# Second attention: scores of two query tiles as 64-row products in both halves of the TensorE array, keys block-diagonal for pairs of heads

## The reference, cut to what matters

```python
def _L1_xattn_ref(x, cond, wq, bq, wkv, bkv, wp, bp):     # x, cond: 16 x 128 x 512
    q = _qdq(x) @ _qdq(wq).T + bq                          # int8 fake-quantised
    k, v = jnp.split(cond @ wkv.T + bkv, 2, axis=-1)
    q, k, v = (t.reshape(B, 128, 16, 32) for t in (q, k, v))
    attn = jax.nn.softmax(jnp.einsum('bnhd,bmhd->bhnm', q, k) * scale, axis=-1)
    o = jnp.einsum('bhnm,bmhd->bnhd', attn, v).reshape(B, N, C)
    return _qdq(o) @ _qdq(wp).T + bp
x = x + _L1_xattn_ref(_layernorm(x), ctx_2048, ...)
```

## Time and profile before

| what | value |
|---|---|
| median of three runs | 1466.27 us |
| the runs | 1461.33, 1466.27, 1466.6 us |
| span of the profiled execution | 1463.7 us |
| second attention, first to last score product | 768.1 to 1037.4 us of the span |
| PE busy over the span | 93% |
| DVE, ACT busy over the span | 69%, 54% |

### The profile page before, as it was taken

One profiled execution on the slowest core, in us unless ns is written; L12 is line 12 of the kernel. 1 busy time (PEld: TensorE's weight loads), 2 busy tenths in 40 slices (PEclk: granted clock), 3 DMA queues, 4 the chain that ended last, 5 costly groups with the idle time before them and its releaser, 6 DMA issues. The chain is left out here.

```text
span 1463.7 us, 28639 instructions
## 1 busy us (share of the span) xinstructions
PE 1354.5 (93%) x8666; PEld 813.1 (56%) x8666; DVE 1002.8 (69%) x3234; ACT 791.5 (54%) x1802; POOL 249.2 (17%) x265
## 2 busy tenths in 40 slices
PE   3678999999999799999989999999789999999998
PEld 1345555555555444444455555555434777777774
DVE  8889999999997646456546788887659654545211
ACT  4777888888888733332357677776530233332331
POOL 4100000000000100000010000002411255555552
PEclk7699999999999999999999999999999999999999
DMA  8534344343440300000020000000322588888885
GB/s 261 145 87 99 91 107 106 86 119 90 107 104 17 145 1 0 0 0 0 0 75 15 16 16 14 14 1 2 146 85 93 184 247 251 255 257 246 255 233 115
DMA packets 63186, 149.52 MB, mean 102 GB/s; under 512 B 10792, under 2 KB 27830, under 8 KB 58892
## 3 DMA queue, kind: packets, MB, share of 16 engines
q1 hardware_dynamic: 49836, 115.70, 26.1%
q0 software_dynamic: 13280, 32.93, 9.6%
HBM read 113.21 MB, written 35.39 MB: 102 GB/s over the span
## 5 line engine op out<-in xcount | busy, mean ns | idle before, releaser
L776 DVE CUSTOM_DVE_ANT_0 masked_scores<-ps_max,band_mask 128x192 bf16<-128x192 f32 (+1 forms) x512 | 177.2, 383 | 20.5 <-PE ps_max L505 13.9
L383 ACT ACTIVATE probs_t<-ps_sc 128x448 f32<-128x448 f32 x256 | 138.7, 542 | 80.4 <-PE ps_sc L525 78.1
L1255 PE MATMUL f_ps<-f_xt,w_t 128*128 (+1 forms) x704 | 160.2, 382 | 2.5 <-ACT w_t L1310 2.5
L377 ACT ACTIVATE nf_above<-nf_scaled,nf_sign_at 128x512 f16<-128x512 bf16 x231 | 161.5, 715 | 0.0
L2803 DVE TENSOR_TENSOR d_inter<-d_silu_g,d_su 128x384 f32<-128x384 f32 x32 | 17.7, 554 | 159.6 <-PE d_su L2487 154.4
L1927 ACT ACTIVATE c_probs<-d_sg,c_negmax 128x128 f32<-128x128 f32 x256 | 90.3, 365 | 58.1 <-DVE c_negmax L2012 57.7
L1255 PEld LDWEIGHTS f_ps<-f_xt,w_t 128*128 128x128 bf16 x704 | 69.3, 98 | 86.7 <-issue 5.0
L2320 POOL DMA_INDIRECT out<-d_h,d_scatter_now x64 | 97.2, 1519 | 108.3 <-DMA out<-d_h,d_scatter_now 92.9
L505 PE MATMUL ps_max<-k_stack,q_stack 96*128 96x192 bf16 (+1 forms) x512 | 96.5, 272 | 19.8 <-DVE row_max L776 13.8
L2671 DVE TENSOR_SCALAR d_onehot<-d_slot_no,d_pos 128x192 bf16<-128x192 bf16 x512 | 101.0, 288 | 0.3 <-PE d_lb L2388 0.3
L505 PEld LDWEIGHTS ps_max<-k_stack,q_stack 96*128 96x128 bf16 x512 | 46.2, 101 | 92.1 <-issue 46.9
(11 more groups left out here) (381 smaller groups left out, 2830.1 us busy)
## 6 DMA issues: line engine op xcount, KB each, us to landing
d_wgu<-in_ex_gu SPq DMA_DIRECT2D x32, 1024.0 KB
d_wdown<-in_ex_d SPq DMA_DIRECT2D x32, 512.0 KB
dr_parts<-qk_parts SPq DMA_DIRECT2D x32, 384.0 KB, 4.8
q_stack<-dr_parts SPq DMA_DIRECT2D x32, 192.0 KB, 2.7
k_stack<-dr_parts SPq DMA_DIRECT2D x32, 192.0 KB, 3.3
out<-x_sb SPq DMA_DIRECT2D x21, 256.0 KB, 2.2
nf_w<-in_nf_w POOLq DMA_DIRECT2D x3, 1408.0 KB, 10.2
q_stack<-dr_parts SPq DMA_DIRECT2D x32, 128.0 KB, 2.4
```

The lines of the kernel that those rows point to most:

```text
L377: act.activation(above[:, g, k, :], lvl[:, g, :], ACT.Sign, bias=cut[:, k - NDV:k - NDV + 1]).then_inc(s_sg, 1)
L383: act.activation(pt[:, c, :], SP[c % 2][:].rearrange("p a w -> p (a w)")[:, a:z], ACT.Exp, scale=D0 ** -0.5).then_inc(s_e, 1)
L776: op = dve.tensor_tensor_reduce(masked[:, c % 2, k, off:off + hi - lo], M[c % 2][:, k, off:off + hi - lo], mask[:, k, off:off + hi - lo], ...
L1255: mm = pe.matmul(bank[:], w12[:, m, kt, ft * P:(ft + 1) * P], xt[:, q, kt, bass.ds(g * N, N)], start=(kt == 0 and q == 0), stop=(kt == KT ...
```

## The change

One product of scores now covers two heads instead of four: the keys in `kbd` are block-diagonal only within pairs of heads, so a tile of 128 features by 128 keys shrinks from four key blocks (512 columns) to two (256 columns), and rows 0 to 63 and rows 64 to 127 are used by separate products, each with 64 rows and 256 columns. `score_pair` issues the four of them for two neighbouring tiles, `ot` and `ot + 1`: those of the lower half of the rows write bank `SB[0]`, those of the upper half bank `SB[1]`. A bank therefore holds two heads of two tiles. The pair waits until all exponentials before it are done, since it fills both banks. The number of maxima is as before (two for two tiles, each over a whole bank), and so are the exponentials and the transposes; what each exponential reads is another place.

On ScalarE the key copies of steps 0 and 4 now stand behind the exponentials of steps 1 and 5, together with those of these steps (`key_piece`), and `q_bias(g, 1)` behind the exponentials of step 1 instead of step 0. The two buffers of keys are half as large, so the memsets that zero them are too.

```diff
-            def scores(n, par, bb, ot):
-                ge(pe, s_ex, n - 1)
-                pe.matmul(SB[ot % 2][:], qt[:, par, ot, bb * P:(bb + 1) * P], kbd[par][:, ot, bb, :, :],
-                          start=True, stop=True).then_inc(s_S, 1)
+            def score_pair(n, par, bb, ot):
+
+                ge(pe, s_ex, n)
+                for o in range(2):
+                    for a in range(2):
+                        rows = slice(64 * a, 64 * a + 64)
+                        mm = pe.matmul(SB[a][:, 2 * o:2 * o + 2, :], qt[rows, par, ot + o, bb * P:(bb + 1) * P],
+                                       kbd[par][rows, ot + o, bb, :, :], start=True, stop=True, skip_group_check=True)
+                        if o == 1:
+                            mm.then_inc(s_S, 1)
...
-                        if bb == 0 and ot % 2 == 0:
-                            pe.wait_ge(s_qb, 2 * g + ot // 2 + 1)
-                        scores(n, par, bb, ot)
+                        if ot % 2 == 0:
+                            if bb == 0:
+                                pe.wait_ge(s_qb, 2 * g + ot // 2 + 1)
+                            score_pair(n, par, bb, ot)
...
-                    op = act.activation(kbd[par][rows, ot, :, j, :],
+                    op = act.activation(kbd[par][rows, ot, :, j % 2, :],
...
-                        act.wait_ge(s_nm, n + 1)
+                        if ot % 2 == 0:
+                            act.wait_ge(s_nm, n + 1)
                         ge(act, s_T, n - 1)
...
                         for j in range(4):
-                            op = act.activation(pr[:, ot % 2, j, :], SB[ot % 2][:, j, :], ACT.Exp, bias=nm[:, ot % 2, j:j + 1],
+                            if ot % 2 == 0 and j == 2:
+                                act.wait_ge(s_nm, n + 2)
+                            at = 2 * (ot % 2) + j % 2
+                            op = act.activation(pr[:, ot % 2, j, :], SB[j // 2][:, at, :], ACT.Exp, bias=nm[:, j // 2, at:at + 1],
                                                 accum_out=sm[:, bb, 4 * ot + j:4 * ot + j + 1])
                         op.then_inc(s_ex, 1)
-                        if ot == 0 and bb == 0:
+                        if ot == 1 and bb == 0:
                             q_bias(g, par, 1)
                         if ot == 1 and not start:
                             o_copy(i - 1)
                         if not last:
-                            piece(g + 1, 1 - par, 4 * bb + ot)
+                            rows_piece(g + 1, 4 * bb + ot)
+                            if ot % 2 == 1:
+                                key_piece(g + 1, 1 - par, 4 * bb + ot - 1)
+                                key_piece(g + 1, 1 - par, 4 * bb + ot)
...
             def take_max(n, ot):
-                dve.wait_ge(s_S, n + 1)
-                ge(dve, s_ex, n - 1)
-                dve.tensor_reduce(nm[:, ot % 2, :], SB[ot % 2][:], AX.X, ALU.max, negate=True).then_inc(s_nm, 1)
+                ge(dve, s_ex, n)
+                for a in range(2):
+                    dve.wait_ge(s_S, n + a + 1)
+                    dve.tensor_reduce(nm[:, a, :], SB[a][:], AX.X, ALU.max, negate=True).then_inc(s_nm, 1)
```

More of the change, by code:

```diff
@@ L1053, in first_key_tiles @@
 def first_key_tiles(T):
-    return T["wn"][:].bitcast(F32)[:, 0:KT * 2 * 4 * P].rearrange("p (o b j c) -> p o b j c", o=KT, b=2, j=4)
+    return T["wn"][:].bitcast(F32)[:, 0:KT * 2 * 2 * P].rearrange("p (o b s c) -> p o b s c", o=KT, b=2, s=2)
 def load_context(sp, T, I, W, g, par):
@@ L1497, in phase_layer1_attention @@
     qt = sb("c_q_t", [P, 2, KT, GN], F32)
-    kbd = [first_key_tiles(T), sb("c_k_diag", [P, KT, GB, 4, P], F32)[:]]
+    kbd = [first_key_tiles(T), sb("c_k_diag", [P, KT, GB, 2, P], F32)[:]]
     free_k = sb("c_next_rows", [P, 8 * D], F32)
@@ L1868, in q_bias, with rows_piece @@
                 op.then_inc(s_qb, 1)
[L1870 to L1876, removed]
+            def rows_piece(g, k):
+                if k == 3:
                     xq_copy(g, 0)
@@ L1883, in piece, with key_piece @@
                         act.activation(std[:, EARLY:NB], mv[:, EARLY:NB, 1:2], ACT.Sqrt, bias=T["eps"][:, 0:1]).then_inc(s_std, 1)
+            def key_piece(g, par, k):
+                if k == 0:
+                    k_copy(g, par, 0)
+                elif k == 1:
+                    k_copy(g, par, 1)
+                elif k == 4:
                     k_copy(g, par, 2)
@@ L1898, in _ @@
             for k in range(8):
-                piece(0, 0, k)
+                rows_piece(0, k)
+                key_piece(0, 0, k)
                 if k == 1:
@@ L2088, in body @@
                             out_scale(i - 2, bb)
-                        take_max(n, ot)
+                        if ot % 2 == 0:
+                            take_max(n, ot)
                         if ot == 0 and bb == 0:
```

## The result

| | before | after |
|---|---|---|
| median of eleven runs each, us | 1466.27 | 1473.83 |
| lowest and highest, us | 1460.72, 1468.15 | 1469.28, 1476.64 |
| span of the profiled execution, us | 1463.7 | 1471.7 |

The ratio is 1.0061, 95% interval 1.0048 to 1.0073: slower by 7.6 us, where 5.7 was predicted (1472.0) with the time inside the range.

A forecast was written before the change was run, and what follows sets the result against it. PE bounds the kernel (39.6 of 40 us busy in the second attention). Per group 2.6 us more idle less 1.8 saved is + 0.8; seven groups + 5.6, span 1469.3, median 1472 us; likeliest case 1466 to 1478.

The forecast's parts named there:

- The price of the pair: Score products on PE: a pair in row halves takes 1.27 us against 1.72, saving 0.45, or 1.8 per group.
- (c): Score pair on PE: the row halves don't overlap, 0.86 us more per pair, total 1490 us; chance 0.09.
- (b): Score pair on PE: switching is hidden, the waits stay; pair costs 1.0 us, total 1464; chance 0.13.
- (d): Score pair on PE: a half's weight loads wait for its own passes, + 0.33 us per pair, total 1479; chance 0.05.
- The waits: PE waiting in the second attention: idle 3.0 us per group, less the 0.4 of now, + 2.6.
- turn of step 6: PE, second half of a group: this turn waits about 2.1 us for ACT, against 0.40 before.
- pair of step 5: PE, second half of a group: 0.4 us idle, as ACT's step 5 exponentials wait for the `oq_turn` copy.
- query product: PE, second half of a group: this product waits 0.1 us for the third key copy.
- pair behind step 7: PE at the next group's pair: 0.4 us idle while ACT does the query bias and step 7's exponentials.
- Rival (a): Second attention: PE's saving arrives, the waits don't; 13 us less, 1453, or 1442 with free switching; chance 0.14.
- Rival (e): Second attention: ACT's or DVE's chain is 1 us per group longer than counted, total 1479 us; chance 0.07.
- The last group: Last group of the second attention: paced by POOL's 17.1 + 8.2 us for twelve rows whatever PE does, change 0.

The follow-up runs named there:

- e2: The changed kernel with each pair as two full-array products of 128 rows and 512 columns, keys over four heads: 1479.61 us, ratio 1.0087 to before.
- e7: e5 with full-array products of 128 rows and 512 columns in the pair, keys over four heads: 1472.99 us, ratio 1.0043 to before.
- e1: The kernel before, full-array products kept, with only ScalarE's order of the changed kernel (key copies and second query bias later): 1481.96 us, ratio 1.0098.
- e5: e4 plus the next group's first query bias moved behind the exponentials of step 7: 1460.25 us, ratio 0.9967 to before.
- e6: The changed kernel with step 6's output turn issued four times instead of once, 12 more transposes per group: 1470.94 us, ratio 1.0035 to before.
- e4: The changed kernel with the key copy of step 4 back behind the exponentials of step 4: 1472.97 us, ratio 1.0041 to before.
- e3: The changed kernel with step 6's output turn issued five times instead of once, 16 more transposes per group: 1477.23 us, ratio 1.0077 to before.
- e8: The same kernel as e3, run once more for its profile, against the changed kernel: 1478.23 us (one run).

## Why the prediction was right, and where it wasn't

**The price of the pair** held. Predicted 1.27, measured 0.09 + 1.07 + 0.04 = 1.20 (the 0.04 is the turn's surplus); e2 and e7 give 0.5 saved per pair for the 0.45 predicted. The products start in twos 7 ns apart, as foreseen, so (c), halves that don't overlap, is out; (b) would have had the pair at 1.0. In the pair the second, third and fourth twos start 0.32, 0.54 and 0.75 us after the first: only the first is 0.10 longer than 0.215, so the loads of a half hide under that half's own passes, and (d) is out. The Trainium skill (TensorE: Matmul & The Clock Gate, The mechanism) says in one line that a weight load overlaps running products only where the row groups differ; these rows disagree with it, and the measurement decides. The same section also names a background weight buffer as a second case, which the prediction left out.

**The waits** held nearly one by one. At the turn of step 6: 2.1 predicted, 1.97 measured; at the pair of step 5: 0.4 and 0.31; at the query product: 0.1 and 0.16; at the pair behind step 7: 0.4 and 0.19. One of 0.20 at the key products, for DVE's copy of the values, wasn't in the list. Sum 3.0 predicted, 2.83 measured. A group at full clock is 35.46 for the 35.7 predicted: + 0.5 against before, not + 0.8. e1 shows that this comes from the order on ACT, which alone makes + 2.3. Waits of the turn came to 13.8 us, just under the 15 to 20 named. Rival (a), the saving without the waits, is out: e5 is the closest to it, and takes another order. Rival (e), a chain longer by 1 us per group, is out too, since the waits came to less than predicted.

**The term that was missing** is the clock. I took every pass at 0.43 or 0.215 for granted, though the step put 2 us of idle time into an engine that had 0.4 us of it per group. 3 x 1.3 = 3.9 us of the five groups' 6.8 are falls of the clock, and a fourth fall lies behind the last mark, 5.2 us in all. The granted clock of 0.66 behind the wait shows it, and e6 bears it out. The Trainium skill tells of such a thing (same page, HAM oscillation): waits between bursts of products can bring the clock back to its lower level. The waits it describes are longer than this one, so the page taken by itself would not have given the term; the measurement decides.

**The last group** I put at 0, since POOL's 25 us pace it "whatever PE does". They do (25.0 us, 25.3 before), but not when they begin. POOL waits for a reciprocal on DVE that stands behind the maxima of the last group's first pair:

```profile
1018.25 1.29 DVE L2032 TENSOR_REDUCE c_negmax<-d_sg 128x4 f32<-128x512 f32 x2 [1.74 <-PE d_sg L1709]
...
1022.55 0.22 DVE L2134 RECIPROCAL c_next_rstd<-c_next_std 128x12 f32<-128x12 f32 x1
```

That pair comes after the seventh group's wait of 1.97 and, in this trace, at the lower clock (it takes 1.63 us, from 1016.46 to 1018.09). So POOL starts 3.3 us later. In e6, whose wait there is 0.67 and whose clock stays up, it starts 21.2 behind its mark (1014.11 - 992.95), 2.4 more than before; in e5 20.1 (1006.66 - 986.60), 1.3 more. The seventh group's own waits, which the sum did count, thus reach the end through POOL's start; what it lacked there is the fall.

**The sum, term by term.** The marks cut the groups in their middle, and the waits lie in the second half of a group. Up to the mark of 819.46 the prediction's terms have seven pairs, - 3.2, and the waits of the first group, + 2.6: - 0.6. The five groups have + 4.0. Behind the last mark stand one more pair and the seventh group's waits, + 2.2, and 0 for the last group. That is the + 5.6. The span came as - 1.4, + 6.8, + 3.3 and + 0.3, less the 1.0 by which this trace was ahead before the first pair: 8.0. Of it 5.2 are four falls that the sum had not. Without them the terms make 3.8 for the 5.6 forecast, 1.8 too much. So the sum was closer than its terms, and that is partly luck: terms too high by 1.8 and a head start of 1.0 hid 2.8 of the 5.2.

## What to carry to other kernels

When a change puts a wait on a full engine, ask two things beside its length: what comes next in line once this wait is mended (e4), and what else hangs on the engine staying busy (its clock, and here POOL's start). A gain on the bound engine and the order that makes room for it are two changes: in the first order the halves gained 5.8 us and the order cost 13.3 (e2), in the better one they gained 12.7 and it cost 6.8 (e7). What turned 0.6% slower into 0.3% faster was moving two pieces of ACT out of the way of exponentials that PE waits for: the key copy to where ACT had been waiting anyway, the query bias behind the exponentials.

## What I had not expected of the hardware

- TensorE's granted clock fell from 2.4 to 1.2 GHz behind four of seven waits of 1.97 us with the same instructions around them (after), behind four of five of about 1.9 (e4) and behind one of 1.83 among full-array products (e2), but behind none of 1.49 (e2). A fall cost 1.3 us, and work that does nothing, put into the wait, took the falls away (e6).
- Two programs that differ by 4 transposes per group differ by stops that end with no event: 1.5 to 2.0 us in one group and 4.7 to 5.0 us in the last stage (e3 and e8), against one of 0.86 in the last stage (e6). Their cause is open: a control that only adds instructions can cost something far from where it adds them.
